# Matmuls of constants inside the second and the fourth token norm of a hybrid network

## The reference, cut to what matters

```python
def _ln_t(v, eps=1e-05):
    m = jnp.mean(v, axis=-1, keepdims=True)
    s = jnp.var(v, axis=-1, keepdims=True)
    return (v - m) / jnp.sqrt(s + eps)

t = t + _L2_attn_ref(_ln_t(t), ...)   # first token norm
t = t + _L2_ffn_ref(_ln_t(t), ...)    # second, ahead of the mixture of experts
t = t + _L3_attn_ref(_ln_t(t), ...)   # third
t = t + _L3_ffn_ref(_ln_t(t), ...)    # fourth, ahead of the routed blocks
```

## Time and profile before

| | us |
|---|---|
| median of 3 runs | 572.61 |
| lowest, highest | 571.94, 576.02 |
| the profiled execution | 572.74 |
| its span, first to last instruction | 570.9 |
| busy in the span: PE, DVE, ACT, POOL | 503.4, 409.6, 311.7, 158.4 |

### The profile page before, as it was taken

One profiled execution on the slowest core, in us unless ns is written; L12 is line 12 of the kernel. 1 busy time (PEld: TensorE's weight loads), 2 busy tenths in 40 slices (PEclk: granted clock), 3 DMA queues, 4 the chain that ended last, 5 costly groups with the idle time before them and its releaser, 6 DMA issues. The chain is left out here.

```text
span 570.9 us, 15184 instructions
## 1 busy us (share of the span) xinstructions
PE 503.4 (88%) x6313; PEld 293.7 (51%) x6313; DVE 409.6 (72%) x751; ACT 311.7 (55%) x543; POOL 158.4 (28%) x210
## 2 busy tenths in 40 slices
PE   8957778999888889989888878989999999999993
PEld 3547654466665553255555544444664566366520
DVE  5758978686444589967788857975786776777664
ACT  3255635243344310267988875355776577667573
POOL 0106423000000000043565640000692078038600
PEclk9976899999999879999999999979999999999998
DMA  8400007000000075000000000000000000000002
GB/s 262 47 6 3 3 2 242 1 2 1 2 1 2 1 175 121 0 3 1 2 1 2 3 20 2 0 8 13 1 3 6 8 2 1 12 2 2 1 7 77
DMA packets 22560, 15.02 MB, mean 26 GB/s; under 512 B 17466, under 2 KB 20570, under 8 KB 22363
## 3 DMA queue, kind: packets, MB, share of 16 engines
q1 hardware_dynamic: 22490, 14.00, 9.8%
HBM read 8.71 MB, written 1.08 MB: 17 GB/s over the span
## 5 line engine op out<-in xcount | busy, mean ns | idle before, releaser
L2327 DVE TENSOR_REDUCE R<-ps 128x4 f32<-128x1024 f32 x48 | 56.6, 1221 | 21.3 <-PE ps L1849 20.9
L2150 ACT ACTIVATE R<-ps 128x512 f32<-128x512 f32 x96 | 52.0, 597 | 11.0 <-PE ps L1861 10.9
L2233 POOL TENSOR_TENSOR R<-R 128x512 f32<-128x512 f32 x42 | 53.3, 1270 | 16.4 <-ACT R L2150 16.4
L1609 POOL TENSOR_TENSOR R<-R 128x512 f32<-128x512 f32 x32 | 45.4, 1417 | 39.8 <-DVE R L1542 39.8
L1542 DVE TENSOR_TENSOR R<-ps,lasting 128x512 f32<-128x512 f32 x64 | 41.1, 685 | 11.7 <-PE ps L1464 11.7
L1861 PE MATMUL ps<-tmpA,R 32*128 32x256 f32 x384 | 48.3, 378 | 0.0
L1576 ACT ACTIVATE R<-R 128x1536 f32<-128x1536 f32 x32 | 47.3, 1479 | 0.1
L1849 PE MATMUL ps<-R,tmpA 32*128 32x256 f32 x384 | 45.4, 392 | 0.0
L1464 PE MATMUL ps<-R,Q 32*128 32x128 f32 (+1 forms) x512 | 29.9, 346 | 10.0 <-ACT R L1592 10.0
L1861 PEld LDWEIGHTS ps<-tmpA,R 32*128 32x128 f32 x384 | 36.5, 185 | 0.5
L1464 PEld LDWEIGHTS ps<-R,Q 32*128 32x128 f32 x512 | 23.9, 184 | 20.8 <-DVE R L1542 16.9
(11 more groups left out here) (336 smaller groups left out, 1103.9 us busy)
## 6 DMA issues: line engine op xcount, KB each, us to landing
R<-z SPq DMA_DIRECT2D x32, 128.0 KB, 2.4
R<-in_qv SPq DMA_DIRECT2D x1, 2560.0 KB
x<-in_x SPq DMA_DIRECT2D x4, 256.0 KB, 3.5
out<-x SPq DMA_DIRECT2D x4, 256.0 KB, 2.6
lasting<-in_lasting SPq DMA_DIRECT2D x1, 811.0 KB, 8.4
early<-in_early SPq DMA_DIRECT2D x1, 793.5 KB, 7.0
scatter<-in_scatter SPq DMA_DIRECT2D x1, 512.0 KB, 5.4
P<-scratch_w SPq DMA_DIRECT2D x16, 32.0 KB, 2.6
```

What stands on the lines that cost most here:

```text
L1609: pool.tensor_tensor(diagonal(u), diagonal(u), diagonal(u), ALU.mult).then_inc(diag_squared[1], 1)
L2150: act.activation(m.et[:, g % 2, j, :], ps[:, turned_bank(g, j), :], ACT.Exp)\
L2233: pool.tensor_tensor(m.esum[:, g % 2, two, :], m.et[:, g % 2, two, 0:N], m.et[:, g % 2, two, N:2 * N], ALU.add).then_inc(sg["halves_added" ...
L2327: dve.tensor_reduce(m.parts[:, g % 2, :, a:a + 2, 3 * g].rearrange("p s i -> p i s"), ps[:, a:a + 2, :].rearrange("p i (s m) -> p i s m", ...
```

## The change

A function `turn_over` is added at the level of the file: it issues n matmuls of 128x512 in bf16 on `m.scatter` (a table of constants) into a bank of PSUM. Its results are not read: the bank is written anew, or not used any more. `token_norm` has a new argument `filled`, which is on for the second and the fourth token norm. With it TensorE issues

- one such matmul behind the gathering of each of the chunks 0, 1 and 2 (into bank 2),
- three behind the gathering of chunk 3, ahead of the wait for the first reciprocal (bank 2),
- two ahead of the wait for the second reciprocal, behind a wait for the centring of all four chunks (bank 5, from which DVE reads a mean).

The semaphore of the first half is still raised by the last gather of chunk 1. In the first token norm and the attention norm nothing changes, and no other engine's instructions do.

```diff
--- before.py
+++ after.py
@@ -101,7 +101,14 @@
         pe.matmul(m.ps[:, bank, :], t[:, 0:128], t[:, 0:CH], start=True, stop=True)
 
 
-def token_norm(m, sem, name, parts, outs, eps, mean_w, gamma=None, ready=None):
+def turn_over(pe, m, bank, n):
+
+    t = m.scatter[:, :, :].rearrange("p g n -> p (g n)").bitcast(BF16)
+    for _ in range(n):
+        pe.matmul(m.ps[:, bank, :], t[:, 0:128], t[:, 0:CH], start=True, stop=True)
+
+
+def token_norm(m, sem, name, parts, outs, eps, mean_w, gamma=None, ready=None, filled=False):
 
 
 
@@ -138,8 +145,18 @@
                     for i in range(n):
                         mm = gather_squares(pe, m, VAR_BANK[half], sq[i], g, g % GH == 0 and i == 0,
                                             g % GH == GH - 1 and i == n - 1)
-            mm.then_inc(var_ready, 1)
+                if filled and k < NCH - 1:
+                    if k % 2:
+                        mm.then_inc(var_ready, 1)
+                    turn_over(pe, m, 2, 1)
+            if not filled or half:
+                mm.then_inc(var_ready, 1)
+        if filled:
+            turn_over(pe, m, 2, 3)
         for half in range(2):
+            if filled and half:
+                pe.wait_ge(centred, NCH)
+                turn_over(pe, m, 5, 2)
             pe.wait_ge(inverted, half + 1)
             for g in range(GH * half, GH * half + GH):
                 for q in range(QN):
@@ -1218,7 +1235,7 @@
     def turned_gates(half):
         return ps[:, (1, 7)[half], :].bitcast(BF16)
 
-    norm = token_norm(m, sem, "ln2", [m.x], [m.z], EPS_T, m.blkmean)
+    norm = token_norm(m, sem, "ln2", [m.x], [m.z], EPS_T, m.blkmean, filled=True)
     after = m.after_experts
 
     with nc.Block() as block:
@@ -1619,7 +1636,7 @@
     both = ((1, m.pa), (0, m.sa))
 
     last_norm = token_norm(m, sem, "ln4", [m.x], [m.h], EPS_T, m.blkmean,
-                           ready=lambda eng, k: eng.wait_ge(summed, NCH + k + 1))
+                           ready=lambda eng, k: eng.wait_ge(summed, NCH + k + 1), filled=True)
     def run_pe(pe):
         norm.pe(pe)
         for w, (i, _) in enumerate(both):
```

## The result

| | before | after |
|---|---|---|
| median of 4 runs each, us | 572.28 (567.55 to 576.02) | 579.12 (576.59 to 581.31) |
| ratio, 95% interval | | 1.0128 (1.0084 to 1.0171) |
| profiled execution, its span, us | 572.74, 570.9 | 576.59, 574.8 |
| forecast, us | | 573.9 (572.0 to 576.0) |

Single executions of one kernel lie up to 6 us to either side of their mean, so each side is also pooled over the runs of this study: a mean of 573.8 us before (108 runs, 567.4 to 579.8), 579.5 after (22 runs, 574.1 to 585.7). By that the change costs 5.7 us; lot by lot the medians differ by 6.8, 7.8 and 4.5. All ratios leave out executions recorded as slow (over 1.5% above the fastest of their kernel) and aren't the plain quotients of the medians.

A forecast was written before the change was run, and what follows sets the result against it. DVE's small steps were taken to bound the stretch behind the second norm, TensorE at half clock the one behind the fourth. Profiled 572.74 + 1.6 (second norm) - 0.45 (fourth) = 573.9 us, range 572.0 to 576.0.

The forecast's parts named there:

- Second norm, +1.6 at L1319: Second norm: fillers delay the logits and DVE's expert choice from L1319 on by 1.6 us (0.8 to 1.6).
- lone filler with changing over: Filled norms: one filler between two gathers costs 0.45 us, 0.216 its own and 0.23 for changing over.
- spreading 0: Second norm, sign of being right: the first spreading starts some 3.2 us after the first gather instead of 1.87.
- Rival 1: Both norms: fillers cost only 0.216 us each and the clock stays; sum 572.3 us, chance 0.2.
- rule on row groups: Filled norms: a weight load passes running matmuls only if its row group differs, so a filler would not pass a gather.
- A faster clock there is worth about 0: Behind the second norm: TensorE's slow stretch lies wholly under DVE's row of small steps, so full clock gains about 0.
- If the clock stays full ... Fourth norm: -0.45: Fourth norm and first routed block: at full clock the norm's delay is more than won back, net -0.45 us.
- Rival 2: First routed block: the fall is put off to between 377.8 and 382, +1.0 us there; sum 575.3, chance 0.25.
- slow 10.1 us: Behind the fourth norm: half-clock stretch from 377.6 to 387.7 us, taken as the most a faster clock could work on.
- Rival 3: Fourth norm: the clock falls at 377.5 as before and the full delay stays, +1.6+2.0; sum 576.3, chance 0.08.
- Rival 4: Ahead of the attention norm, about 340 us: the fall grows (+1.0, 574.9) or vanishes (-1.7, 572.2); chance 0.07.
- Two more falls on the path: Anywhere on the path: what being slower by over 1%, 578.3 us, would need; chance 0.02.

The follow-up runs named there:

- ln2_second3: Fillers in the second norm only, second keep_busy cut from six matmuls to three, against the kernel before: ratio 1.0026 (0.9995 to 1.0058).
- first8_again: Repeat of ln2_first8 on another chip, against the kernel before: ratio 1.0008 (0.9970 to 1.0046).
- after_second3: The full change with the second keep_busy cut from six matmuls to three, against the kernel before: ratio 1.0034 (1.0005 to 1.0062), 577.75 us.
- ln2_first8: Fillers in the second norm only, first keep_busy raised from five matmuls to eight, against the kernel before: ratio 1.0013 (0.9976 to 1.0051).
- ln4_and_pauses: Kernel before plus fillers in the fourth norm and the eight fillers of pauses, second norm unfilled: ratio 0.9960 (0.9926 to 0.9994), 573.96 us.
- ln4_only: The change with fillers in the fourth norm only, against the kernel before: ratio 1.0049 (1.0018 to 1.0080).
- pauses: Kernel before plus five fillers ahead of the first up projection and three behind the first hidden token, norms unfilled: ratio 0.9984, 571.93 us.
- before_again: The kernel before, unedited, run again for a second trace: ratio 0.9982 (0.9950 to 1.0014).
- ln2_delay: Kernel before without fillers, three unused DVE sums added ahead of the second norm's first reciprocal: ratio 1.0102 (1.0057 to 1.0146).
- ln2_only: The change with fillers in the second norm only, against the kernel before: ratio 1.0060 (1.0018 to 1.0102).
- after_again: The changed kernel, unedited, run again, against the kernel before: ratio 1.0140 (1.0089 to 1.0192).
- after_third: The changed kernel, unedited, run a third time, against the kernel before: ratio 1.0096 (1.0053 to 1.0140), 579.67 us.

## Why the prediction was wrong

**Second norm, +1.6 at L1319: right, a little high.** Measured +1.40 in all eight traces with that norm filled (10.28 or 10.30). The price of a lone filler with changing over came out as sized (0.69 us for 16 records and one filler, predicted 0.70), groups of three and two a little cheaper, spreading 0 started 3.17 us behind the first gather (3.2), the logits 1.41 later (1.6). Rival 1's cheap filler is refuted by the 0.69. (The rule on row groups that the prediction takes from the Trainium skill, TensorE: Matmul & The Clock Gate, stands there in Part 3 under The mechanism, not under the heading that it names.)

**"A faster clock there is worth about 0": the step that failed in the second norm.** It asked what the slow clock costs *where it was*, and that is nothing; it didn't ask what a full clock sets off. The first keep_busy is then through in 4.54 us instead of 7.16, TensorE is idle for 2.53, and the clock falls on the second keep_busy, which overruns DVE. Cost +1.2 to +1.6 in the stage to L261, in the four traces with that fall and six matmuls. ln2_second3 shows the overrun to be the loss (29.21 with the fall still there), first8_again that without a fall there is no loss either. That the idle 2.53 us brings the fall is supported by first8_again and by after_second3's second fall behind an idle 2.28, and not shown: ln2_first8 fell elsewhere. Nor do the fillers always keep the first keep_busy at full clock: in two of eight traces (after_second3, ln2_first8) the fall came 10 us behind the centring, as without them.

**"If the clock stays full ... Fourth norm: -0.45": the step that failed there.** The condition doesn't hold; the sum behind it does. In ln4_and_pauses, where the clock did stay full, centring to mask takes 20.52 against 20.91 in before (5.06 + 8.18 + 7.67), which is -0.39. Rival 2 came out almost as written, with a fall at the second up projection (384.8) and a loss of 0.74 between the two profiled executions (it said 1.0). The prediction gave it 0.25 for the right reason, the pause without a filler, and should have given it more, since the attention norm, unfilled, had kept the clock while the pause in front of the routed block hadn't. (That norm too was read on one execution: in ln4_only and ln2_first8 the clock fell right behind it.) The trace of pauses settles it: fillers in the pauses alone end the fall.

**The size of the fourth norm: one execution taken as the kernel.** The slow 10.1 us of the earlier trace rows were this execution's. The other traces have 7 us, and against before_again the fillers' loss is 2.1 to 2.2, not 0.74. Against it even a full clock doesn't pay for the delay: 20.52 - 19.52 = +1.0.

**Rival 3** (the clock falls as before) didn't come. **Rival 4** did, as -1.54 in the stage to the attention norm (it said -1.7), but +1.41 ahead of the first attention row, where the clock is at 0.50 at 251.7, took it back. Both came in all three traces of after, and neither needs fillers: ln2_delay has both, while ln2_only has neither. What brings the fall at 57 us stays open.

**Sum and range.** Measured stages: 1.4 + 1.6 + 2.1 (against the 7 us stretch), and the two at 251 and 340 that nearly cancel: 5.1 of the pooled 5.7; what is left, 0.6, is within the spread. The range ended at 576.0 because each case held one mishap; the result was rival 2 *and* a new wait *and* an execution of before that flattered the change. "Two more falls on the path" for the slow side, at 0.02, comes nearest to it, and was priced far too low.

## What to carry to other kernels

Try constant matmuls that are to hold TensorE's clock in the pauses ahead of the slow stretch before putting them in front of work on the path; in this kernel eight of them in two pauses ended a fall that eight in the fourth norm only put off. A keep_busy that was sized on a slow clock is too short on a fast one, and one sized on a fast clock is too long on a slow one: before the clock changes over such a stretch, work out both lengths against the engine that it bridges. Read two or three traces of the kernel before pricing a clock effect, since the length of a slow stretch differs between executions of one kernel.

## What the runs showed of the hardware

- A slow stretch can be moved without being shortened: in after, after_again, after_third, after_second3 and ln4_only it came 11 us behind the fourth norm's first centring instead of 7, and stayed about 7 us long.
- A fall costs by where it lies. On the first keep_busy of five matmuls it cost nothing (29.21 in before, before_again, pauses and ln4_and_pauses), some 7 us of it up to and on the second one of six 1.2 to 1.6 us, ahead of the first attention row 1.4 to 1.7, behind the attention norm 2.4 to 2.5.
- In ln2_delay DVE's three sums of 1.62 us in all moved L1319 by 2.8 us: 1.17 of it came as delay, 1.65 as logits at 0.50.
- The spread of one kernel's runs isn't fixed: before's 35 runs beside pauses reached from 567.7 to 579.0 us, pauses' 12 from 570.6 to 573.3. The filled pauses don't explain that, since ln4_and_pauses has the same and reached from 569.6 to 580.7.
- Much of the spread sits ahead of everything studied here: the second norm's first centring starts anywhere from 191.5 us (after_third) to 199.9 (first8_again), with the same code ahead of it in all of them; behind the mask, 179.1 to 179.8 us are left in every trace.
